# Three banks for the plain convolutions, a smaller early shift, later reads and a later store in a fused convolution and sign-product kernel

## What is computed

```python
out = lax.conv_general_dilated(x, weight, window_strides=(1,), padding=[(4, 4)],
                               dimension_numbers=('NCH', 'OIH', 'NCH'), feature_group_count=4)  # 9 taps, 64 channels, 4 groups
ctx = jnp.einsum('nd,od->no', cond_128, c_weight)         # 32 x 64
y = out + ctx[:, :, None] + bias[None, :, None]
w = kernel.astype(x.dtype) * 2.0 - 1.0                    # 1024 x 1024, true/false to +1/-1
result = x + scale * jnp.einsum('bsi,if->bsf', y, w)
```

## Time and profile before

| | us |
|---|---|
| median of 3 runs | 171.03 |
| lowest and highest run | 170.11 and 171.05 |
| the profiled execution | 170.11 |
| its span in the trace | 168.3 |
| PE busy in the span | 162.8 |
| VectorE busy | 137.0 |
| ScalarE busy | 71.5 |
| POOL busy | 40.1 |

### The profile page before, as it was taken

How to read it: one execution, slowest core, us unless ns; L and a number is a source line. 1 busy time by engine, 2 the same in 40 slices (tenths; PEclk the granted TensorE clock), 3 DMA queues, 4 the chain that set the end, 5 groups by cost and what they waited for, 6 DMA issues and landing times.

```text
span 168.3 us, 2770 instructions
## 1 busy us (share of the span) xinstructions
PE 162.8 (97%) x918; PEld 136.3 (81%) x918; DVE 137.0 (81%) x180; ACT 71.5 (42%) x65; POOL 40.1 (24%) x47
## 2 busy tenths in 40 slices
PE   7999999999999999999999999999999999999992
PEld 2469889898888779888998889887998879888782
DVE  4827567978999999779986999779977999779843
ACT  3327493570991058423772079124762071204100
POOL 5621820005130424006400433014400622000000
PEclk9999999999999999999999999999999999999999
DMA  5889489777899878697898879897988682806024
GB/s 201 252 183 321 117 230 189 181 105 186 140 344 250 255 144 314 136 245 210 214 306 206 238 143 356 182 268 132 318 219 220 102 275 64 186 0 246 7 86 164
DMA packets 27037, 33.38 MB, mean 198 GB/s; under 512 B 3536, under 2 KB 19344, under 8 KB 27024
## 3 DMA queue, kind: packets, MB, share of 16 engines
q1 hardware_dynamic: 21600, 25.36, 55.7%
q10 hardware_dynamic: 4912, 6.78, 15.0%
q0 software_dynamic: 512, 1.07, 2.8%
HBM read 10.06 MB, written 8.40 MB: 110 GB/s over the span
## 4 chain that ended last, share of the span: by engine, by line
PE 90%; DMA 4%; DVE 3%; issue 1%; ACT 1%; DVEq 0%; ACTq 0%
PE ps_A L845 30%; PE ps_conv L826 19%; PE ps_C L845 16%; PE ps_conv L801 8%; PE ps_B L845 8%; PE ps_C L861 2%; PE ps_B L861 2%; PE ps_toep L861 2%; PE ps_A L861 2%; DMA x_nat<-x 2%; DMA x_blk<-x_phase 2%; PE ps_C L787 1%; DVE x_nat L663 1%; ACT x_phase L245 1%; DVE x_nat L649 0%
## 5 line engine op out<-in xcount | busy, mean ns | idle before, releaser
L491 ACT CAST hi<-sums 128x1024 fp32r<-128x1024 f32 x14 | 14.7, 1049 | 42.1 <-DVE sums L628 30.5
L410 POOL TENSOR_TENSOR set<-x_blk 128x512 f32<-128x512 f32 x12 | 16.2, 1366 | 68.0 <-DMA x_blk<-x_phase 68.0
L649 DVE SCALAR_TENSOR_TENSOR x_nat<-ps_A,scale_col,x_nat 128x512 f32<-128x512 f32 x27 | 20.2, 749 | 13.8 <-PE ps_A L845 12.9
L448 ACT COPY x_phase<-x_nat 128x1032 f32<-128x1032 f32 x13 | 27.2, 2133 | 2.9 <-issue 2.9
L491 ACT CAST hi<-y_sum 128x1024 fp32r<-128x1024 f32 (+1 forms) x14 | 11.7, 833 | 27.8 <-DMA y_sum<-y_two 21.6
L845 PE MATMUL ps_A<-sign_T,hi 128*128 128x512 f32 x80 | 22.3, 400 | 0.0
L845 PE MATMUL ps_A<-sign_T,lo 128*128 128x512 f32 x80 | 21.8, 395 | 0.0
L845 PEld LDWEIGHTS ps_A<-sign_T,lo 128*128 128x128 f32 x80 | 15.1, 189 | 3.5
L826 PE MATMUL ps_conv<-toeplitz,w_bytes 128*128 128x128 f32 x144 | 17.2, 276 | 0.4 <-DVE y_two L602 0.4
L826 PEld LDWEIGHTS ps_conv<-toeplitz,set 128*128 128x128 f32 x144 | 16.9, 192 | 0.7 <-issue 0.2
L410 POOL TENSOR_TENSOR w_bytes<-x_blk 128x512 f32<-128x512 f32 x12 | 12.3, 1049 | 21.2 <-DVE sums L628 11.2
(11 more groups left out here) (108 smaller groups left out, 238.6 us busy)
## 6 DMA issues: line engine op xcount, KB each, us to landing
x_nat<-x SPq DMA_DIRECT2D x16, 512.0 KB, 4.4
out<-x_nat SPq DMA_DIRECT2D x15, 512.0 KB, 4.9
x_blk<-x_phase SPq DMA_DIRECT2D x114, 64.5 KB, 2.9
y_sum<-y_two ACTq DMA_DIRECT2D x48, 128.0 KB, 3.4
w_bytes<-w_bool SPq DMA_DIRECT2D x2, 512.0 KB, 5.9
x_blk<-x_phase POOLq DMA_DIRECT2D x8, 64.5 KB, 3.2
shift<-shift_dram POOLq DMA_DIRECT2D x2, 256.0 KB, 6.8
x_blk<-x_phase ACTq DMA_DIRECT2D x6, 64.5 KB, 4.8
```

The costliest lines, as they stand in the source:

```text
L410: nc.gpsimd.tensor_tensor(dif[r][:, e], x_blk[r][:, :, e:e + M:2], x_blk[r][:, :, e + 1:e + 1 + M:2][:, :, 0:K], ALU.subtract).then_inc(di ...
L448: nc.scalar.copy(x_phase[r][:, :, 0:M + 1], line(d, r, 0, PAD + L + PAD).rearrange("r (m q) -> r q m", q=B)).then_inc(phase_ok[r], B)
L491: nc.scalar.copy(parts(hi_all, k), group(k)).then_inc(hi_ok[k], 1)
L649: nc.vector.scalar_tensor_tensor(there, bank[b], scale2_col[:, :], there, ALU.mult, ALU.add).then_inc(summed[k], 1)
```

## The change

1. A tensor `offset` of 32 float32 a partition (128 bytes) is put ahead of `w_bytes`, so that `w_bytes`, the signs and everything behind them lie 128 bytes further in SBUF. It is not used otherwise.
2. `EARLY` is 4 instead of 8: the early matmul makes the shifts of double 0 alone. Those of double 1 come by two new DMAs on POOL's queue, with a semaphore `next_in` that double 1's adds wait for.
3. PE's Toeplitz transposes start when half of the taps are spread, and wait for the other half after four of them.
4. The plain convolutions take their banks in turn from all three of `ps_conv` (`part`), and wait for the add three halves back.
5. On VectorE the two reads of double 1's products P2 and P1 follow the y of the next double's first pair; the plain sum of bank E goes behind both y; the read C22_C goes ahead of the second half of the T4 signs.
6. On ScalarE the odd copy of double 2's first pair goes ahead of the cast of S1 and S2.
7. On SP the store of double 0's second pair goes from step 0 to step 1, behind the block DMAs and loads there.

```diff
-EARLY = 8
+EARLY = 4
...
+        offset = sb("offset", [P, 32])
         w_bytes = sb("w_bytes", [P, B, L], mybir.dt.uint8)
...
-        shift_0 = sb("shift_0", [P, EARLY, C])
+        shift_0 = sb("shift_0", [P, 2 * EARLY, C])
...
+        def part(d, r, i):
+            return ps_conv[:, (4 * d + 2 * r + i) % 3]
...
+                if d == 1:
+                    store(0, 1)
                 store(d, 0)
                 if last(d):
                     store_last(d)
-                else:
+                elif d > 0:
                     store(d, 1)
...
             pool.wait_ge(shift_out, 16)
             for i in range(2):
+                pool.dma_start(shift_0[:, EARLY + i:2 * EARLY:2],
+                               shift_by_image[i:i + 1, 2:4].to_broadcast([P, 2, C])).then_inc(next_in, 16)
+            for i in range(2):
...
+                odd_blocks(2, 0)
                 high_part("S12", 1)
-                odd_blocks(2, 0)
...
-                if i == 0:
+                if i == 0 and d == 0:
                     dve.wait_ge(early_ok, 1)
+                elif i == 0:
+                    dve.wait_ge(next_in, 32)
...
                 for k in s_sum:
                     combine(k, 1)
-                plain_sum("E")
                 low_part("S12", 1)
...
-                sum_up("C11_P2", d)
-                sum_up("C11_P1", d)
+                if d > 1:
+                    sum_up("C11_P2", d)
+                    sum_up("C11_P1", d)
                 if runs(d, 2):
                     fast_y(d + 1, 0)
+                if d == 1:
+                    sum_up("C11_P2", d)
+                    sum_up("C11_P1", d)
                 low_part("A22", d)
                 if runs(d, 2):
                     fast_y(d + 1, 1)
                 if d == 1:
+                    plain_sum("E")
                     last_signs(slice(0, KH // 2))
...
                     sum_up("C12_A", d)
                     low_part("S34", d)
+                    sum_up("C22_C", d)
                     if d == 1:
                         last_signs(slice(KH // 2, KH))
-                    sum_up("C22_C", d)
                     sum_up("C22_A", d)
...
-            pe.wait_ge(exp_ok, 2)
+            pe.wait_ge(exp_ok, 1)
             for s in range(2):
                 for u in range(B):
+                    if (s, u) == (0, B // 2):
+                        pe.wait_ge(exp_ok, 2)
...
-                    if r == 1 or d > 0:
-                        pe.wait_ge(y_ok, 8 * d + 4 * r + 2 * h - 2)
+                    if 4 * d + 2 * r + h > 2:
+                        pe.wait_ge(y_ok, 2 * (4 * d + 2 * r + h - 2))
...
-                            now = nc.tensor.matmul(ps_conv[:, h, g].rearrange("m u o -> m (u o)"),
+                            now = nc.tensor.matmul(part(d, r, h)[:, g].rearrange("m u o -> m (u o)"),
```

More of the change, by code:

```diff
@@ L172, in conv_product_kernel @@
             sem, ("ident_zero", "ident_ok", "taps_zero", "pads_ok", "scale_ok", "early_done", "early_ok"))
+        next_in = sem("next_in")
         exp_ok, toep_done, toep_ok, small_done, small_ok, ctx_done, shift_ok, shift_out = map(
@@ L561, in _ @@
             dve.wait_ge(early_done, 1)
-            nc.vector.tensor_copy(shift_0[:, :, :].rearrange("m n o -> m (n o)"), ps_early).then_inc(early_ok, 1)
+            nc.vector.tensor_copy(shift_0[:, 0:EARLY].rearrange("m n o -> m (n o)"), ps_early).then_inc(early_ok, 1)
             def sign_sums(k, left, op, right, u=slice(0, KH)):
@@ L583, in add_shift @@
                     nc.vector.tensor_tensor(
-                        y_sum[r][:, i, u].rearrange("m u (g o) -> m g u o", g=GROUPS), ps_conv[:, i, :, u],
+                        y_sum[r][:, i, u].rearrange("m u (g o) -> m g u o", g=GROUPS), part(d, r, i)[:, :, u],
                         shift_0[:, 4 * d + 2 * r + i].rearrange("m (g o) -> m g o", g=GROUPS).unsqueeze(2)
```

## The result

| | before | changed |
|---|---|---|
| median of 20 runs, us | 170.62 | 169.31 |
| lowest and highest | 169.56 and 171.47 | 167.56 and 172.16 |
| ratio, 95% interval | | 0.9904 (0.9877 to 0.9930) |
| the profiled execution and its span | 170.11, 168.3 | 169.69, 167.8 |

The forecast was 170.9 on a median of 171.03, so 0.1 us less. The measured difference is 1.3 us by the medians and 1.6 by the ratio. The ratio leaves out executions over 1.5% above the fastest of their kernel, three of the changed kernel's 20, and the profile of the kernel with the 128 bytes alone, further down, is of such an execution (171.59 us).

A forecast was written before the change was run, and what follows sets the result against it. PE, busy 97% of the span, was taken as the bound. Gains of 0.80 + 0.72 + 0.35 = 1.87 us, mostly given back through VectorE, left -0.1: 170.9 us on a median of 171.03, range 169.1 to 172.0.

The forecast's parts named there:

- The 128 bytes: Moving the signs 128 bytes in SBUF: the forecast counted no effect on the product matmuls.
- The signs' place changes the matmul: Rival: the signs' SBUF place speeds all products by 7.3 us, to 163.6; a fifth gives 169.5; chance 0.07.
- The start: Early matmul and first plain convolutions on PE: fewer columns, no wait for VectorE's first add; 0.80 us gained.
- Fast convolutions of the second double: PE's wait there for VectorE's first add of y goes: 6.08 us becomes 5.36, gain 0.72 us.
- P3: Product P3 of the second double: VectorE reads its bank before half of the T4 signs; gain 0.35 us.
- Where it is given back: VectorE's gap-free list loses 1.11 us, so P7 and next P1 wait; of 1.87 us gross, -0.1 us net remains.
- the two ends -0.57 and +0.24: Net change in us at the next step's P1: -0.57 if S1 runs free, +0.24 if not; middle -0.1 taken.
- VectorE becomes the bound: Rival: GpSimd's differences hold S1 in steps 3 and 4 too, P1 waits in each; slower, 172.2 us; chance 0.15.

## Why the prediction was wrong

**The 128 bytes: the step that failed.** The sum had "I take nothing" for the 128 bytes. Alone they give 1.1% (ratio 0.9891, 1.9 us), and all the rest without them nothing that can be told (0.9984), so this term was wrong, and the chance of 0.07 for "The signs' place changes the matmul" far too low. I saw that the product's 0.232 us lies 0.016 over the warming matmul's 0.216 and had no reason for it in the profile; then I took it for a constant, because all products had it. They all had it because the pieces of the high parts, low parts and signs that a matmul takes follow each other at multiples of 256 bytes (512 and 2048), so every product has the same distance modulo 256. That was in the code, and was the reason why one shift of 128 bytes changes all of them. As a size the rival was too large: a third of the 0.016 went, 0.0054, so 2.5 us of TensorE time and not 7.3; the 169.5 us that I gave for a fifth of it lies close to the 169.31 measured. The Trainium skill (SBUF — State Buffer, Specifications) counts lines of 16 bytes. By that alone 64, 128, 144 and 160 bytes, all whole lines, would be alike; the runs give 5.60, 5.44, 5.60 and 5.60, and the measurement decides.

**The start: right.** Forecast 0.80 us. The kernel without the 128 bytes begins its first product at 17.35 in the chain against 18.17: 0.82, of which 0.09 is that the first convolution began sooner (8.69 against 8.78).

**Fast convolutions of the second double and P3: right.** Forecast 0.72. Without the 128 bytes they run from 42.95 to 48.22, 5.27 us, against 6.00 from start to start before (43.77 to 49.77). P3 starts without a wait.

**Where it is given back: right, to a tenth.** VectorE's timeline of the kernel without the 128 bytes, in which the other parts of the change are alone:

```profile
44.03 0.69 DVE L615 TENSOR_TENSOR y_two<-ps_conv,shift 128x512 f32<-128x512 f32 x1 [0.27 <-PE ps_conv L845]
...
52.26 0.75 DVE L662 SCALAR_TENSOR_TENSOR x_nat<-ps_A,scale_col,x_nat 128x512 f32<-128x512 f32 x1
...
57.92 1.54 DVE L641 TENSOR_TENSOR sums<-y_sum 128x512 f32<-128x512 f32 x1
...
60.65 0.74 DVE L662 SCALAR_TENSOR_TENSOR x_nat<-ps_A,scale_col,x_nat 128x512 f32<-128x512 f32 x1
```

and its chain:

```profile
61.54 2.10 PE ps_A L864 x8
63.64 5.36 PE ps_conv L845 x48
```

The first addition was put at 44.07 at the soonest, the read of P6 at 52.30, the read of P4 at 60.71, the end of P1 at 63.66. They came at 44.03, 52.26, 60.65 and 63.64. One wait was put too high: VectorE waits 0.27 us for PE ahead of the first addition, not 0.64. Its four combinations took 4.13 us from the first start to the next operation, where they took 3.77 before, since two of them took 1.34 and 1.54 (1.18 and 1.36 before), and so it reached the addition later. The end is the same because PE's result sets it either way. The three additions took 2.40 us from the first start to the next read, as forecast (46.46 less 44.07). S1 didn't run free, so of the two ends -0.57 and +0.24 it was the second in this profile. The time without the 128 bytes, ratio 0.9984 (0.9955 to 1.0013), is as good as unchanged, which is what the forecast's 0.1 us said of these parts.

**VectorE becomes the bound: wrong for the change, right as a mechanism.** The time went down. Of the rival's condition, that GpSimd's differences hold S1 in steps 3 and 4 too, half came: S1 took 1.53 in step 3 (76.36) instead of 0.69, and 0.68 in step 4. Without the 128 bytes P1 waits 0.57, 0.08, 0.06 and 0.08 us in steps 2, 3, 5 and 6; with the faster product it waits 1.17, 0.20, 0.21 and 0.21, since PE comes sooner and VectorE doesn't. That is 1.0 us of the product's gain that doesn't arrive.

## What to carry over

Where every matmul of a kind is a little slower than the same shape elsewhere in the trace, look at the distance of its two SBUF operands, and try a few sizes of padding between them: it costs a line, and one profile shows the result in the spacing of the rows (what it gives in time takes more executions). Test an edit that seems to do nothing by itself before pricing it at nothing. And when a wait names one instruction in a list that has no gaps, take work out of the list; changing the order within it moves the wait to whoever stood behind.

## What the runs showed of the hardware

- A matmul of 128 x 512 with float32r operands (TensorE at full granted clock) comes every 0.2321 us (signs moved by 0 or 256 bytes against the operands), every 0.2333 (by 64, 144 or 160) or every 0.2267 (by 128 or 384). The distance in SBUF between the stationary operand and the moving one decides; moving both together by 128 bytes left 0.2321. Where matmuls at the good distance and at the other take turns in fours, nearly all of the gain is lost (5.56 us for 24, against 5.44 and 5.57). The plain convolutions' passes of 128 columns kept their 0.112 us in all these kernels; the operands of the fast ones were never moved against each other. Why this is so, no run here tells.
- GpSimd's and VectorE's operations with two SBUF inputs hold each other up: a low part of 128x512 took 1.85 us beside GpSimd instead of 0.68, and S1 1.54 instead of 0.68; GpSimd's two differences took 3.26 us (from 56.86, with the plain sum of E later) instead of 2.05.
